# A graph layer with residual layernorm: the first turn fetches one half of its tiles through the DMA queue alone

## The reference

```python
h = x[src]                                    # 103125 x 64
def step(m, rw):                              # over the 16 types
    r, w_r = rw
    mask = jnp.where(etypes == r, 1.0, 0.0)
    return m + mask[:, None] * (h @ w_r), None
m, _ = jax.lax.scan(step, zeros, (arange(16), weight))
out = layernorm(x + segment_sum(m, dst, 3125), axis=-1)
```

## Time and profile before

| | |
|---|---|
| median of 3 runs | 776.13 us (774.11 to 776.22) |
| the profiled execution | 776.07 us, with a span of 774.3 us |
| busy: PE | 698.0 us, 90% |
| busy: DVE | 661.0 us, 85% |
| busy: ACT | 635.1 us, 82% |
| busy: POOL | 549.9 us, 71%, of it 529.1 us in 558 fetches at L324 |

### The profile page before, as it was taken

One profiled execution on the slowest core, in us unless ns is written; L12 is line 12 of the kernel. 1 busy time (PEld: TensorE's weight loads), 2 busy tenths in 40 slices (PEclk: granted clock), 3 DMA queues, 4 the chain that ended last, 5 costly groups with the idle time before them and its releaser, 6 DMA issues.

```text
span 774.3 us, 25434 instructions
## 1 busy us (share of the span) xinstructions
PE 698.0 (90%) x8821; PEld 673.4 (87%) x8822; DVE 661.0 (85%) x2221; ACT 635.1 (82%) x1232; POOL 549.9 (71%) x588
## 2 busy tenths in 40 slices
PE   1888999999999999999899998999999899999955
PEld 1578999999999999999898998989899898989955
DVE  4998798889989888898988899898898989899824
ACT  5866898988889898888979889888888879888713
POOL 2665677777777777777777777777777777777760
PEclk9979999999999999999999999999999999999985
DMA  8321333322332232233222222223223222222211
GB/s 206 89 73 53 73 70 77 80 74 73 79 81 72 74 79 80 66 82 78 68 78 81 65 82 78 72 74 81 72 74 78 80 66 82 76 70 65 54 51 43
DMA packets 29950, 59.01 MB, mean 76 GB/s; under 512 B 11624, under 2 KB 11874, under 8 KB 29930
## 3 DMA queue, kind: packets, MB, share of 16 engines
q0 software_dynamic: 18368, 37.65, 18.4%
q1 hardware_dynamic: 11254, 20.29, 10.0%
q10 hardware_dynamic: 308, 0.80, 0.5%
HBM read 56.30 MB, written 2.40 MB: 76 GB/s over the span
## 4 chain that ended last, share of the span: by engine, by line
POOL 62%; issue 24%; DVE 6%; PE 4%; DMA 1%; ACT 1%; POOLq 1%; ACTq 0%; DVEq 0%
POOL rows L324 61%; DVE pick L522 3%; PE own L747 3%; POOL rows L320 2%; DMA x_sb<-in_x 1%; DVE onehot L589 1%; PE own L891 1%; DVE outT L631 0%; PE agg L782 0%; DMA rows<-x_parts,gidx 0%; DVE x_sb L663 0%; POOLq L76 0%; ACT pick L414 0%; DVE src_f L577 0%; DVE src_f L579 0%
## 5 line engine op out<-in xcount | busy, mean ns | idle before, releaser
L324 POOL DMA_INDIRECT rows<-x_parts,gidx x558 | 529.1, 948 | 194.8 <-issue 174.0
L747 PE MATMUL own<-xp,pick 125*128 125x192 bf16 x5800 | 503.2, 248 | 44.0 <-ACT pick L414 21.0
L747 PEld LDWEIGHTS own<-xp,pick 125*128 125x128 bf16 x5800 | 482.1, 99 | 62.4 <-issue 50.3
L522 DVE TENSOR_SCALAR pick<-src_h,node 125x516 bf16<-125x516 f16 (+1 forms) x1240 | 465.8, 455 | 39.0 <-ACT src_h L376 38.9
L408 ACT ACTIVATE away<-src_h,node_neg 125x516 bf16<-125x516 f16 (+1 forms) x310 | 195.1, 692 | 1.8
L414 ACT ACTIVATE pick<-away,one 125x516 bf16<-125x516 bf16 (+1 forms) x310 | 194.6, 692 | 0.0
L589 DVE TENSOR_SCALAR onehot<-ramp,krel 128x112 bf16<-128x112 bf16 x806 | 148.8, 261 | 0.0
L782 PE MATMUL agg<-onehot,rows 128*128 128x112 bf16 x2418 | 133.4, 214 | 13.1 <-DMA rows<-x_parts,gidx 12.0
L782 PEld LDWEIGHTS agg<-onehot,rows 128*128 128x128 bf16 x2418 | 124.2, 99 | 18.2 <-issue 15.9
L423 ACT ACTIVATE rows<-own 128x384 bf16<-128x384 f32 x124 | 58.2, 470 | 89.6 <-PE own L747 89.3
L388 ACT ACTIVATE aggT<-agg 64x512 f32<-64x512 f32 x124 | 72.7, 586 | 14.5 <-PE agg L782 13.0
(11 more groups left out here) (66 smaller groups left out, 83.3 us busy)
## 6 DMA issues: line engine op xcount, KB each, us to landing
src_b<-in_src SPq DMA_DIRECT2D x62, 258.0 KB
rows<-x_parts,gidx POOLq DMA_INDIRECT x574, 2.5
x_parts<-xp SPq DMA_DIRECT2D x1, 728.0 KB
x_parts<-xp SPq DMA_DIRECT2D x1, 672.0 KB
out<-x_sb SPq DMA_DIRECT2D x2, 224.0 KB
x_sb<-in_x ACTq DMA_DIRECT2D x1, 364.0 KB
x_sb<-in_x ACTq DMA_DIRECT2D x1, 336.0 KB
src_i<-in_src SPq DMA_DIRECT2D x1, 312.0 KB
```

What stands on the lines that cost most here:

```text
L324: pool.indirect_dma_start(rows[:, u, j, :], None, x_parts, bass.IndirectOffsetOnAxis(ap=gidx[:, u, j:j + 1], axis=0)).then_inc(rows_in[u] ...
L522: v.tensor_scalar(pick[u][:, b, 0:CUT * cut_width(u, odd)], src_h[u][:, :, 0:cut_width(u, odd)], node[:, b:b + 1], None, ALU.is_equal).the ...
L747: return nc.tensor.matmul(own_slot(u, h), pick[u][:, b, h * P:(h + 1) * P], xp[:, b, 0:SPLIT, :].rearrange("p s d -> p (s d)"), start=(b = ...
```

## The change

In the first turn PE fetches no tile of u = 1. POOL fetches all thirteen: the three that PE had (`first_in`), the fourth and the nine others. So the u = 1 tiles of `src_b`, `src_h` and `pick` are first used in turn 1, and all their counts become those of `own_turns(i, u) = i - u`. SP no longer spreads the sources of group (0, 1); it spreads those of (1, 0) and (1, 1) behind the stores of `x_parts` and ahead of the weights. On DVE the picks of group (1, 0), which are 516 wide, stand where the 384 wide ones of (0, 1) stood. On ACT the work on (1, 0) moves ahead in the same way. On PE `fetch_own(1, 0)` stands between the two aggregations of turn 0. In every turn ACT's `act_picks(i + 1, 0, 3)` now precedes `group_indices(i + 1, 0)`. The loop bodies hold an even and then an odd turn, where they held an odd and then an even one.

The core of the diff; left out are the new semaphore, the same change of counts in `take_pair`, and two edits in paths that the data here don't reach or that only follow the counts.

```diff
...
             assert LAST % 2 == 0
-            if first == 0:
-                body(0, False)
-            with eng.Fori(0, LAST // 2 - 1) as k:
+            for i in range(first, 2):
+                body(i, i % 2 == 1)
+            with eng.Fori(1, LAST // 2) as k:
+                body(k * 2, False)
                 body(k * 2 + 1, True)
-                body(k * 2 + 2, False)
-            body(LAST - 1, True)
             if last > LAST:
...
+        def own_turns(i, u):
+            return i - u
+        def has_own(i, u):
+            return not (is_first(i) and u == 1)
+        def first_own(i, u):
+            return isinstance(i, int) and i == u
         def cut_width(u, odd):
...
-                if not is_first(i):
-                    sp.wait_ge(src_h_ready[u], i)
+                if not first_own(i, u):
+                    sp.wait_ge(src_h_ready[u], own_turns(i, u))
                 a = src[bass.ds(i * (2 * ROW) + u * ROW, OWNW[u])]
...
             load(et_i, etype, et_in, far_i[:, :])
-            spread_sources(0, 1)
             pv = x_parts.rearrange("(p b) d -> p b d", b=NB)
...
                 spread_sources(i, 1)
+            spread_sources(1, 0)
+            spread_sources(1, 1)
             for q in range(2):
...
             sp.dma_start(par_row[:, :], par[:, :]).then_inc(par_in, 16)
-            group_loop(sp, turn, first=1)
+            group_loop(sp, turn, first=2)
             with go_general(sp):
...
                 pool.nop(nofuse=True)
+                if not has_own(i, u):
+                    for j in range(FEWER):
+                        pool.indirect_dma_start(
+                            rows[:, u, j, :], None, x_parts,
+                            bass.IndirectOffsetOnAxis(ap=gidx[:, u, j:j + 1], axis=0)).then_inc(first_in, 16)
                 if own_count(u, odd) == FEWER:
...
             def narrow_sources(i, u, odd):
-                act.wait_ge(src_b_in[u], (i + 1) * 16)
-                if not is_first(i):
-                    act.wait_ge(pick_ready[u], i * VPICK)
-                    act.wait_ge(act_pick_ready[u], i)
+                act.wait_ge(src_b_in[u], (own_turns(i, u) + 1) * 16)
+                if not first_own(i, u):
+                    act.wait_ge(pick_ready[u], own_turns(i, u) * VPICK)
+                    act.wait_ge(act_pick_ready[u], own_turns(i, u))
                 w = cut_width(u, odd)
...
                 if part == 0:
-                    if not is_first(i):
-                        act.wait_ge(own_done[u], i * 2)
-                        act.wait_ge(act_pick_ready[u], i)
-                        act.wait_ge(act_pick_ready[1 - u], i + u)
-                    elif u == 1:
-                        act.wait_ge(act_pick_ready[0], 1)
-                    act.wait_ge(src_h_ready[u], i + 1)
+                    if not first_own(i, u):
+                        act.wait_ge(own_done[u], own_turns(i, u) * 2)
+                        act.wait_ge(act_pick_ready[u], own_turns(i, u))
+                    if u == 1:
+                        act.wait_ge(act_pick_ready[0], i + 1)
+                    elif not isinstance(i, int) or i > 1:
+                        act.wait_ge(act_pick_ready[1], own_turns(i, 1))
+                    act.wait_ge(src_h_ready[u], own_turns(i, u) + 1)
                 cuts = (0, APICK // 2, APICK)
...
                 else:
-                    act.wait_ge(away_ready, i * 4 + (2 * u + part - 1))
+                    act.wait_ge(away_ready, part - 1 if is_first(i) else i * 4 + (2 * u + part - 3))
                     for b in range(b0, b1):
...
             act.activation(et_f[:, :], et_i[:, :], ACT.Copy).then_inc(et_cast, 1)
-            narrow_sources(0, 1, False)
-            act_picks(0, 1, 0, False)
-            act_picks(0, 1, 1, False)
             act.wait_ge(zeros_set, 1)
             clear_agg(0)
+            narrow_sources(1, 0, True)
+            act_picks(1, 0, 0, True)
             take_pair(0, 0, 0, False)
+            act_picks(1, 0, 1, True)
             take_pair(0, 0, 1, False)
-            act_picks(0, 1, 2, False)
-            act_picks(0, 1, 3, False)
             act.wait_ge(krelT_done, 1)
...
             def turn(i, odd, more=True):
-                if more:
+                if more and not is_first(i):
                     narrow_sources(i + 1, 0, not odd)
...
                     take_agg(i - 1, 1)
-                if more:
+                if more and not is_first(i):
                     act_picks(i + 1, 0, 0, not odd)
-                take_pair(i, 1, 0, odd)
-                if more:
+                if has_own(i, 1):
+                    take_pair(i, 1, 0, odd)
+                if more and not is_first(i):
                     act_picks(i + 1, 0, 1, not odd)
-                take_pair(i, 1, 1, odd)
+                if has_own(i, 1):
+                    take_pair(i, 1, 1, odd)
                 if more:
...
                 if more:
-                    group_indices(i + 1, 0)
                     act_picks(i + 1, 0, 3, not odd)
+                    group_indices(i + 1, 0)
                 if more:
...
-                dve.wait_ge(src_h_ready[u], i + 1)
-                if not is_first(i):
-                    dve.wait_ge(own_done[u], i * 2)
+                dve.wait_ge(src_h_ready[u], own_turns(i, u) + 1)
+                if not first_own(i, u):
+                    dve.wait_ge(own_done[u], own_turns(i, u) * 2)
                 for b in range(VPICK):
...
                             shift[:, :].rearrange("g (j o) -> g j o", o=1).to_broadcast([G, GT, P]), ALU.subtract).then_inc(krel_cast, 1)
-            picks(0, 1, False)
+            picks(1, 0, True)
             dve.wait_ge(krel_done, 2)
...
             def turn(i, odd, more=True):
-                if more:
+                if is_first(i):
+                    pass
+                elif more:
                     picks(i + 1, 0, not odd)
...
                 if not is_first(i):
-                    pe.wait_ge(pick_ready[u], (i + 1) * VPICK)
-                    pe.wait_ge(act_pick_ready[u], i + 1)
+                    pe.wait_ge(pick_ready[u], (own_turns(i, u) + 1) * VPICK)
+                    pe.wait_ge(act_pick_ready[u], own_turns(i, u) + 1)
-                if not is_first(i):
-                    pe.wait_ge(own_rows[1], i * 4)
+                if not isinstance(i, int) or i > 1:
+                    pe.wait_ge(own_rows[1], own_turns(i, 1) * 4)
+                elif i == 1:
+                    pe.wait_ge(own_rows[0], i * 4)
                 def product(h, b):
...
                 pe.wait_ge(onehot_ready[u], i + 1)
-                pe.wait_ge(own_rows[u], (i + 1) * 4)
+                if has_own(i, u):
+                    pe.wait_ge(own_rows[u], (own_turns(i, u) + 1) * 4)
+                else:
+                    pe.wait_ge(first_in, 16 * FEWER)
                 for j in range(GT):
...
             def turn(i, odd, more=True):
-                fetch_own(i, 1, odd)
+                if has_own(i, 1):
+                    fetch_own(i, 1, odd)
                 if is_first(i):
...
                     aggregate(i, 0, odd, window_starts(i, 0))
-                    aggregate(i, 1, odd, window_starts(i, 1))
                     fetch_own(i + 1, 0, not odd)
+                    aggregate(i, 1, odd, window_starts(i, 1))
                     pe.wait_ge(w_centered, 2)
```

More of the change, by code:

```diff
@@ L172, in gnn_resnorm @@
         gidx_ready, rows_in, late_in = sem2("gidx_ready"), sem2("rows_in"), sem2("late_in")
-        fourth_in = sem("fourth_in")
+        first_in, fourth_in = sem("first_in"), sem("fourth_in")
         src_b_in, src_h_ready, pick_ready = sem2("src_b_in"), sem2("src_h_ready"), sem2("pick_ready")
@@ L418, in take_pair @@
             def take_pair(i, u, k, odd):
-                act.wait_ge(own_done[u], i * 2 + (k + 1))
+                act.wait_ge(own_done[u], own_turns(i, u) * 2 + (k + 1))
                 pair = own_pair(2 * u + k)
@@ L474, in turn @@
                 if more:
+                    act_picks(i + 1, 0, 3, not odd)
                     group_indices(i + 1, 0)
-                    act_picks(i + 1, 0, 3, not odd)
                 if more:
@@ L683, in _ @@
                         v.tensor_copy(av[:, j0:j1, :], own[m][:, 0:(j1 - j0) * G].rearrange("p (j g) -> p j g", g=G)).then_inc(g_set, 1)
-                dve.wait_ge(own_done[1], (LAST + 1) * 2)
+                dve.wait_ge(own_done[1], LAST * 2)
                 dve.wait_ge(g_set, 5)
@@ L813, in transpose_x @@
                 for u in range(2):
-                    pe.wait_ge(own_rows[u], (LAST + 1) * 4)
+                    pe.wait_ge(own_rows[u], (own_turns(LAST, u) + 1) * 4)
                 for n in range(n0, n1):
@@ L827, in turn @@
                     aggregate(i, 0, odd, window_starts(i, 0))
+                    fetch_own(i + 1, 0, not odd)
                     aggregate(i, 1, odd, window_starts(i, 1))
-                    fetch_own(i + 1, 0, not odd)
                     pe.wait_ge(w_centered, 2)
```

## The result

The changed kernel takes 768.64 us (median of 4 runs, 768.45 to 768.91), the kernel before 775.12 (4 runs, 773.65 to 776.22). The ratio is 0.9918, with a 95% interval from 0.9897 to 0.9939: faster, by 6.5 us where 7.8 were forecast, and at 768.64 where 768.3 was. The profiled execution took 768.91, with a span of 767.1.

The account below looks back on a forecast made before the run. POOL's row of fetches was taken to bound the kernel: 11.6 us of waits removed less 3.75 for three added fetches puts (2, 0) 7.8 earlier. Span 774.3 - 7.8 = 766.5, plus 1.77, makes 768.3 us; range 766.4 to 771.5.

Parts of the forecast that it names:

- The bound: POOL from 81.86 on: a row of 537 fetches, one per 1.25 us, so the start of group (2, 0) decides.
- The removed waits and the added fetches: POOL ahead of (1, 0), (1, 1), (2, 0): 11.6 us of idle goes, three new fetches cost 3.75; (2, 0) 7.8 earlier.
- PE's side: PE's aggregations and fetches of the first turns: POOL may start (2, 0) at 72.7, needed at 74.1, so no wait.
- The one-hot matrices: DVE, first group, behind the wide `picks(1, 0)`: ready at 44.4, 1.4 us later than before; PE waits for them.
- The low stretch: PE at 1.2 GHz after 9 us idle, around `fetch_own(1, 0)`: one stretch costing 1.67 us, bounds 0 and 3.3.
- The gap ahead of `fetch_own(1, 1)`: PE's idle time there shrinks from 2.77 to 0.7 us; start at 59.4, full clock taken, 8.4 long.
- The margin at (2, 0): Group (2, 0) could start at 72.7 by its row numbers and POOL arrives at 74.1: 1.4 us left.
- ACT: ACT's first turn: picks of (1, 0) ready at 43.2, row numbers at 43.4, both ahead of need.
- what lies behind (2, 0): POOL's later groups: no wait behind (2, 0), as before, so the whole 7.8 us gain there stays.
- the tail: From the last fetch to the kernel's end, 752.5 to 774.3 before: untouched by the change, 21.8 us.
- rival D: PE's clock stays at 1.2 GHz through both fetches: 16.8 us more, (2, 0) at 87.8, time 782.1; chance 0.05.
- The unknown of the start: Two `src_b` copies (258 KB each) behind the `x_parts` stores might delay the first fetch 2.3 us (770.6); 0 taken.

Follow-up runs that it names:

- experiment 7: Changed kernel without DVE's second operation of centering `x` (mean not subtracted; a copy of 25 numbers in its place): 767.93 us.
- Experiments 3: Changed kernel with three more indirect DMAs of POOL in group (0, 1), into a tile that nothing reads: 772.42 us.
- experiment 4: Kernel before with three more indirect DMAs of POOL in group (0, 1), into a tile that nothing reads: 775.31 us, ratio 0.9994.
- 8: Changed kernel with PE fetching four u = 1 tiles, not three, in turns 24, 26, 28, 30, POOL one less in each: 764.14 us, ratio 0.9868.
- experiment 2: Changed kernel with PE's `fetch_own(1, 0)` put back behind both aggregations of turn 0: 775.72 us, ratio 1.0011 to the kernel before.
- experiment 5: Changed kernel with the sources of group (1, 1) (258 KB) spread among the first loads, not behind the stores of `x_parts`: 768.97 us.
- Experiment 6: Changed kernel in which PE works out the first tile of `fetch_own(1, 1)` three times, 50 matmuls more: 772.10 us.
- experiment 1: Changed kernel with ACT copying the row numbers of group (i+1, 0) ahead of its last three picks again: 768.34 us.
- the first experiments: Follow-up runs other than those on the two slow chips; the kernel before took 772.78 to 778.02 us over 25 runs, 774.71 the median.

## Why the prediction was right

*The bound.* POOL's fetches set the time, from the first fetch on in the changed kernel, but for the two long ones at the start, whose ends DVE sets (experiment 7). Experiments 3, 4 and 8 show it from three sides: a fetch more costs 1.25 where POOL doesn't wait and nothing where it does, and a fetch less saves about that (1.1).

*The removed waits and the added fetches.* Forecast: 40 fetches in one row, (2, 0) at 74.1. Measured: one row, (2, 0) at 73.46. The 0.6 is the sum of a start 0.96 earlier and the long fetch of 2.40, which was 2.01 in the trace of before; the prediction took these long fetches over with the row and doesn't name them. The order on PE carries all of it (experiment 2).

*PE's side.* The one-hot matrices were at hand at 43.9 (44.4 forecast). The low stretch cost 2.3, where one of 1.67 was taken and 0 to 3.3 were the bounds; the one stretch taken was right in kind, and its size, 1.5 to 2.9 in the traces, was not known. The gap ahead of `fetch_own(1, 1)` was 0.86 (0.7), it started at 59.26 (59.4), and the clock stayed full. The margin at (2, 0) was 1.1 (1.4), and 0.6 in the trace of experiment 5: a longer low stretch within the stated bounds would have used it up. Experiment 6 shows that it is real and how small it is.

*ACT.* The picks of (1, 0) were done at 42.9 (43.2), and the row numbers moved behind the picks cost nothing (experiment 1).

*What was off.* The gain between the medians is 6.5 and not 7.8. The term that failed is what lies behind (2, 0), which was taken as unchanged. From the start of (2, 0) to the end of the last fetch the profiled executions took 670.65 before and 671.66 now, 1.0 more, all of it in the long fetch at 723.89; the tail took 22.0 and not 21.8. Between the profiled executions the gain is 7.2, as the 8.4 at (2, 0) less these. The rest is the kernel before itself: its median over 4 runs is 775.12, over 3 it was 776.13, and over the 25 runs of the first experiments 774.71. The absolute time was forecast to 0.3 us partly by luck, since errors of either sign met: an earlier start against a longer fetch. In rival D the sum in brackets comes to 11.2 and not to 10.8; nothing hangs on it.

*The unknown of the start.* The two copies behind the stores of `x_parts` didn't delay the first fetch: it came earlier, within the spread of the starts. The ring order that the page "DMA: Bandwidth & Descriptors" of the Trainium skill states in the section "Queues, rings and completion order" would give no delay either; no run here shows the order.

## What to carry to other kernels

Where one engine issues transfers at a fixed pace, lay its issues out in time and sum up the waits: instructions added to it cost nothing as long as a wait behind them takes them up, and their full price afterwards. A change that frees such an engine is worth its waits only if the others arrive in time, so work out their margin at each wait; here two aggregations in the wrong order gave all of it back. When the margin grows along the kernel, as PE's did here from about 1 to 7.5 us, move work over to the engine with the margin in the late turns only.

## What the runs showed that was not expected

A POOL fetch that starts beside DVE's operation on `x` with two f32 inputs from SBUF (125x1600, 1.82 us) ends 0.8 after it, and takes 1.43 to 2.53 in nine traces in place of 0.94. A fetch that is already under way isn't held: the one at 732.31 in the kernel before, 0.07 ahead of the operation, took 0.95. Beside DVE's reduction of the same tile, and beside its picks from f16 to bf16, fetches take 0.94. The Trainium skill, "SBUF — State Buffer", section "Who interferes with whom", says that DVE in a two-port mode blocks GpSimd, and that an instruction with two SBUF inputs contends with a GpSimd instruction that reads SBUF; it infers that the making of descriptors is not held up by the second kind. These fetches are held up by it: experiment 7 took the two-input operation away, and the long fetch was gone. They also take their row numbers from the SBUF tile `gidx`, so that the page's rule on reads may cover them; no run separates the reading of the numbers from the making of descriptors. The trace agrees on the reduction, which the page says never contends.

After 9.22 us without work PE did its first 5 us at 1.2 GHz; a gap of 0.86 left the clock at 2.4 GHz. Gaps of near 2.8 went both ways: behind 2.77 the fetch took 10.07 in the kernel before and 9.96 in experiment 4, behind 2.79 it took 8.41 in experiment 2.

On two chips PE waited again and again between single matmuls (0.5 to 1.2 us each in the rows above, 406.5 in all in that trace), and the kernel before took 1.74 and 1.77 times its 775 us. Why was not found.
